# A graph and feed-forward layer: the first-layer products of the feed-forward moved between the two halves of the message sums

## The chip, the core and the metric

The kernel runs on one core of a Trainium2 chip. The metric is the device time of one execution in microseconds (us). The kernel is written with explicit semaphores: each engine (TensorE, VectorE or DVE, ScalarE or ACT, GpSimd or POOL, and SyncE or SP, which issues most DMAs) works through its own queue in program order and waits where the program says so.

## The reference

It is one layer over a graph of 6250 nodes with 256 features and 106,250 edges, sorted by target node.

```
xn = layernorm(x)
# graph attention, 4 heads of 64
h = xn @ W;  e = leaky_relu(a_src[src] + a_dst[dst]);  m = segment_max(e, dst)
ex = exp(e - m[dst]);  alpha = ex / segment_sum(ex, dst)[dst]
g = sigmoid(segment_sum(alpha * h[src], dst) + bias)
# linear attention with a gate
q, k, v = xn @ Wqkv;  k = softmax(k over nodes);  o = q @ (k^T v)
mix = (o * sigmoid(gelu(ln(xn) @ Wg1 + bg1) @ Wg2 + bg2)) @ Wproj + bproj
x = x + g + mix
# feed-forward on the nodes with the 3124 highest router weights of xn2
xn2 = layernorm(x);  r = xn2 @ wr + br
y = (gelu(xn2 @ w1 + b1) @ w2 + b2) * r     (256 -> 1024 -> 256)
out = x + xn2 + (y where selected, else 0)
```

Features, sums and weights are float32.

## The kernel before, in words

The nodes are 49 tiles of 128; the edges are 52 slices of 2048, each of four groups of 512 edges. A first part makes the node features and writes them to DRAM. The main part, on which the change bears, is one loop of 52 rounds over the slices (`steps`, which unrolls rounds 0 to 11 and 50 and 51 and repeats two rounds between). In a round k each engine runs a list of small functions in the order in which its `steps` call writes them out; every entry has a first and a last round. Node work trails edge work: a node tile is merged 5 rounds after its slice (LAG_MERGE), summed up after 6, its feed-forward's first layer runs from round 8 on (LAG_FF1), the second layer one round later.

What a round does for its edges:

- POOL (`fill`, L1014) gathers the feature rows of the next slices, 16 indirect DMAs in four batches g of four. Batch 0 waits for `scores_done` of TensorE, batch 1 for `scores_turned`, batch 2 for `max_turned`, batch 3 for `sums_done` of the first half of the sums. In the order of time a round has batch 3 (behind the first sums), batch 0, then batches 1 and 2.
- TensorE: `turn_scores` (L1824, instructions of L1833) transposes the edge scores; VectorE takes segment maxima by two scans; `turn_maxima` (L1842) transposes them back; VectorE makes differences (L1332, L1336), ScalarE their exponentials (L1615), VectorE the messages (L1352), four instructions, each 4 of the 16 tiles of gathered rows. TensorE sums the messages by target window (`window_sums`, L1873, instructions of L1882) in two halves, `first_sums` and `other_sums`, 16 instructions each. The first half waits for two of the four message products, the second for all four. Then `scores_ahead` (L1817) makes the target scores of the next slice.
- ScalarE, after the exponentials, runs `hidden` (L1670: the GELU of the first layer, four activations, L1675), then `keep_sums` (L1642: copies each half of the sums), `inverse_root` (L1625, L1627), the gates (L1656, L1660) and `keep_turned` (L1668).
- SP stores the copied sums to DRAM (L1091), loads the x tile (L1118) and the node tile (L1107, L1109), for which the stores must have landed.

The first layer of the feed-forward takes node tiles in pairs: 256 columns (two tiles) by 1024 hidden features. A round does half of the 1024, in two groups (`ff1_group`, L1909, instructions of L1917), eight instructions each, since a float32 product is two. In rounds of u = 0 (even k) both groups run in `other_ff1` (16 instructions). In rounds of u = 1 (odd k) the first group runs early, in `first_ff1`, between the transposes of scores and of maxima, and only the second one in `other_ff1` (8 instructions). The groups wait for GELUs of the round before, and the GELUs wait for `ff1_done`.

Of the kernel before, what the change touches and what calls it, by code (L numbers as in the profile page):

```python
# [73 lines left out]
def gps_layer(nc, x, src, dst, W, att_src, att_dst, gnn_bias, Wqkv, Wproj, bproj, ln_g, ln_b, Wg1, bg1, Wg2, bg2,  # L74
# [18 lines left out]
    with ExitStack() as ctx:  # L93
# [853 lines left out]
        def steps(eng, parts_of_body):  # L947

            loop_from = LAG_OUT + 2 + (LAG_OUT % 2)

            def body(k, u):
                for lo, hi, f in parts_of_body:
                    if lo <= (k if isinstance(k, int) else loop_from) < hi:
                        f(k - lo, (u - lo) % 2)
            for k in range(loop_from):
                body(k, k % 2)
            loop_to = NI - 2 - NI % 2
            with eng.Fori(loop_from // 2, loop_to // 2) as half:  # L960
                for u in range(2):
                    body(half * 2 + u, u)
            for k in range(loop_to, NI):
                body(k, k % 2)


        MAXIMUM = lambda f: (0, 1, f)
# [4 lines left out]
        SECOND = lambda f: (1, 5, f)  # L972
        LOAD_MIXER = lambda f: (0, 1, f)
        PREPARE = lambda f: (2, 3, f)
        CLEARS = lambda f: (0, NI - 2 - NI % 2, f)

        CONTEXT = lambda f: (0, 5, f)
        FOLD = lambda f: (5, 6, f)
        ROUNDS = 8

        EDGES = lambda f: (0, NI, f)
        AHEAD = lambda f: (0, NI - 1, f)
        NODE_AHEAD = lambda f: (LAG_MERGE - 1, NT + LAG_MERGE - 1, f)
        MERGE = lambda f: (LAG_MERGE, NT + LAG_MERGE, f)
        SUM = lambda f: (LAG_SUM, NT + LAG_SUM, f)
        LAST = NT + LAG_SUM - 1
        TURN = lambda f: (LAG_SUM, LAST, f)
        HALF = lambda f: (LAG_FF1, LAST, f)
        FF2 = lambda f: (LAG_FF1 + 1, LAST, f)
# [21 lines left out]
        with nc.Block() as block:  # L1011
# [715 lines left out]
            def _(pe):  # L1727
# [269 lines left out]
                def key_products():  # L1997
                    for i in range(EARLY, NT):
                        if i == EARLY + 12:
                            scores(0, 0)  # L2000
                        if i >= 2:
                            pe.wait_ge(S("keys_kept"), i - 1)
                        for t in range(CT):
                            mm = T.matmul(bank[5 + i % 2][:, 0:C], xnT[:, i, t * P:(t + 1) * P], wk_s[:, t, :],  # L2004
                                          start=(t == 0), stop=(t == CT - 1))
                        mm.then_inc(S("keys_done"), 1)

                def maximum(k, u):
# [6 lines left out]
                    for t in range(CT):  # L2015
# [2 lines left out]
                    mm.then_inc(S("max_across"), 1)  # L2018

                key_products()  # L2020
                steps(pe, [EDGES(turn_scores), FOLD(fold_turn), FF2(odd_ff2), HALF(first_ff1), EDGES(turn_maxima), SECOND(context_between), FOLD(fold_context), SUM(project), HALF(other_ff1),
                           EDGES(first_sums), EDGES(other_sums), AHEAD(scores_ahead), MAXIMUM(maximum), PREPARE(prepare), CONTEXT(context),
                           FF2(even_ff2),
                           FOLD(fold), MERGE(mixer), TURN(turn_normed)])
                last_tiles()
# [30 lines left out]
```

## Time and profile before

| | us |
|---|---|
| median of 3 runs (1601.31 to 1608.53) | 1608.32 |
| the profiled execution | 1624.43 |
| its span, from the first to the last instruction | 1622.4 |
| TensorE busy | 1151.6 (71%) |
| VectorE busy | 1021.9 (63%) |
| POOL busy | 854.7 (53%) |
| ScalarE busy | 513.3 (32%) |
| mean granted TensorE clock | 0.82 of full speed |

A line of the timeline has start, duration, engine, line of the program, operation, operands, the number of instructions merged into it, and in brackets the idle time of the engine before it with what ended it ("remote" is a semaphore that came from elsewhere and couldn't be tied to an instruction; "issue" is time for which the profile shows no wait). PE is TensorE. Of matmuls the trace has the start; their end is modelled. The trace lists when instructions ran, and the next instruction on another engine shows when it could see their completion.

### The profile page before, as it was taken

Reading aid. Unit: us, or ns where it says so; the run is one execution under the profiler, and the core shown is the slowest. Engines: PE = TensorE matmul, PEld = TensorE weight load, DVE = VectorE, ACT = ScalarE, POOL = GpSimd, SP = SyncE. Lnnn points to the kernel's source line nnn. Section 1 sums busy time; section 2 is a strip of 40 time slices with the busy share of each in tenths; the row PEclk is TensorE's granted clock in tenths of the full one; section 3 lists DMA queues with packets and bytes.
Section 4 is the critical chain, followed back from the end, with each engine's and each line's share of the span. In section 5 each row is a group of like instructions: output and inputs, shape, how many; then the busy total and the mean of one; then the engine's idle time right before and its main releaser. Section 6 shows DMA issues by size and latency. Waiting matters only on the chain.

```text
span 1622.4 us, 24002 instructions
## 1 busy us (share of the span) xinstructions
PE 1151.6 (71%) x5817; PEld 838.8 (52%) x5817; DVE 1021.9 (63%) x2596; ACT 513.3 (32%) x1155; POOL 854.7 (53%) x891
## 2 busy tenths in 40 slices
PE   6995667765667866777767677775778666776786
PEld 5753454543445554555445545554555544554565
DVE  6862455466666666665766566666666575766678
ACT  4542232103323333332333233333324232323341
POOL 0713455566565566665666565555656555555300
PEclk9997778865877877887779877887788878887889
DMA  9455355555554455455445444545555544444314
GB/s 250 114 107 142 121 146 152 150 138 132 139 135 123 132 129 132 129 129 136 124 129 131 131 122 126 134 121 130 135 132 131 129 129 124 129 123 128 92 32 159
DMA packets 165906, 212.04 MB, mean 131 GB/s; under 512 B 49524, under 2 KB 131252, under 8 KB 165704
## 3 DMA queue, kind: packets, MB, share of 16 engines
q0 software_dynamic: 39984, 110.94, 27.7%
q1 hardware_dynamic: 117570, 97.15, 21.2%
q10 hardware_dynamic: 8306, 3.41, 1.0%
q8 instruction: 19, 0.31, 0.1%
q14 instruction: 27, 0.22, 0.0%
HBM read 165.93 MB, written 45.46 MB: 130 GB/s over the span
## 4 chain that ended last, share of the span: by engine, by line
PE 24%; issue 23%; DVE 14%; another core or an unknown queue 11%; SPq 11%; ACT 3%; DMA 3%; DVEq 1%; POOL 0%; ACTq 0%; POOLq 0%
PE bank L1882 7%; PE bank L1917 5%; PE bank L1854 4%; SPq L1091 3%; SPq L1065 2%; PE bank L1733 2%; DVE ring L1352 2%; PE bank L2004 2%; PE bank L1893 2%; SPq L1051 2%; DVE forth L1320 1%; DVE srow L1323 1%; DVE xnT L1547 1%; DMA lists<-dloc_d 1%
## 5 line engine op out<-in xcount | busy, mean ns | idle before, releaser
L774 POOL DMA_INDIRECT ring<-feat_d,idx x832 | 816.4, 981 | 588.4 <-issue 419.9
L1882 PE MATMUL bank<-ring,hot 128*64 128x265 f32 x1664 | 251.2, 447 | 98.8 <-issue 65.8
L1882 PEld LDWEIGHTS bank<-ring,hot 128*64 128x64 f32 x1664 | 137.1, 157 | 204.2 <-issue 153.6
L1352 DVE TENSOR_TENSOR ring<-ring,bank 128x1024 f32<-128x1024 f32 x208 | 239.9, 1216 | 1.8 <-issue 1.4
L1917 PE MATMUL bank<-late,w_s 128*128 128x256 f32 x768 | 231.4, 462 | 0.4 <-ACT hT L1675 0.4
L1854 PE MATMUL bank<-w_s,hT 128*128 128x256 f32 x720 | 201.9, 443 | 20.8 <-DVE big L1345 15.8
L1917 PEld LDWEIGHTS bank<-late,w_s 128*128 128x128 f32 x768 | 182.5, 242 | 35.9 <-ACT hT L1675 0.5
L1854 PEld LDWEIGHTS bank<-w_s,hT 128*128 128x128 f32 x720 | 159.4, 227 | 52.6 <-DVE big L1345 16.0
L1833 PE MATMUL bank<-ident,lk 128*16 128x128 f32 x208 | 44.2, 352 | 185.2 <-issue 136.7
L1615 ACT ACTIVATE bank<-diff 128x64 f32<-128x64 f32 x52 | 11.8, 228 | 381.3 <-DVE diff L1336 250.3
L1675 ACT ACTIVATE hT<-bank,b_s 128x256 f32<-128x256 f32 x192 | 78.5, 472 | 150.6 <-remote 116.2
L1833 PEld LDWEIGHTS bank<-ident,lk 128*16 128x16 f32 x208 | 17.6, 103 | 202.0 <-issue 150.4
L1656 ACT ACTIVATE sc<-bank,hbg 128x128 f32<-128x128 f32 x98 | 30.5, 362 | 221.8 <-remote 208.2
L1332 DVE TENSOR_TENSOR ring<-bank,lastT 128x64 f32<-128x64 f32 x52 | 11.7, 225 | 129.6 <-remote 73.5
L1842 PE MATMUL bank<-ident,srow 16*128 16x16 f32 x208 | 33.0, 271 | 71.9 <-DVE srow L1323 50.9
L1320 DVE TENSOR_TENSOR_SCAN forth<-brk,bank 16x512 f32<-16x512 f32 x52 | 62.6, 1204 | 30.8 <-PE bank L1833 19.8
L1642 ACT ACTIVATE wout<-bank 128x265 f32<-128x265 f32 x104 | 38.2, 394 | 134.1 <-PE bank L1882 93.4
L1893 PE MATMUL bank<-wproj_s,sc 128*128 128x256 f32 x196 | 73.3, 509 | 6.1 <-DVE three L1424 3.3
L1842 PEld LDWEIGHTS bank<-ident,srow 16*128 16x128 f32 x208 | 28.7, 208 | 94.5 <-issue 94.5
L1389 DVE TENSOR_SCALAR late<-three,bn 128x256 f32<-128x256 f32 x47 | 20.7, 440 | 76.2 <-issue 41.2
L1249 DVE SCALAR_TENSOR_TENSOR sc<-sc,bank 128x256 f32<-128x256 f32 x49 | 20.4, 416 | 74.1 <-ACT sc L1656 74.1
L1267 DVE TENSOR_TENSOR hot<-bank,dlocT 128x512 f32<-128x512 f32 x104 | 66.4, 679 | 0.0
(284 smaller groups left out, 1808.2 us busy)
## 6 DMA issues: line engine op xcount, KB each, us to landing
parts_d<-zero SPq DMA_DIRECT2D x59, 265.0 KB
parts_d<-wout SPq DMA_DIRECT2D x208, 66.2 KB
lists<-dloc_d SPq DMA_DIRECT2D x104, 128.0 KB
ring<-feat_d,idx POOLq DMA_INDIRECT x832
parts<-parts_d SPq DMA_DIRECT2D x49, 265.0 KB
big<-in_x SPq DMA_DIRECT2D x7, 896.0 KB, 10.8
three<-in_x SPq DMA_DIRECT2D x49, 128.0 KB
out<-xnT SPq DMA_DIRECT2D x5, 896.0 KB, 4.2
```

The costliest lines, as they stand in the source:

```text
L774: pool.indirect_dma_start(out=ring[:, u * TI + q, 0:AW], out_offset=None, in_=feat_d, in_offset=bass.IndirectOffsetOnAxis(ap=idx[:, u, q:q ...
L1091: sp.dma_start(part_d[c][bass.ds(first[g], WIN), :], wout[c * WIN:(c + 1) * WIN, n, :]).then_inc(S(f"window_out{g % 2}"), 16)
L1267: V.tensor_tensor(hot[:, tiles, :], iota_ps.unsqueeze(1).to_broadcast([P, 2 * TG, WIN]), dlocT[:, bass.ds(k, 1), tiles].rearrange("p a q - ...
L1320: V.tensor_tensor_scan(forth[:, :], brk[:, 0:GE], bk_t[0:TI, :], LOWEST, ALU.add, ALU.max).then_inc(S("forth_made"), 1)
L1352: V.tensor_tensor(feats, feats, ex[:, g * TG:(g + 1) * TG, :].unsqueeze(3) .to_broadcast([P, TG, HEADS, HD]), ALU.mult).then_inc(S("scaled ...
L1675: A.activation(hT[:, 4 * u + m, :], bank[6 + m // 2][:, m % 2 * 2 * P:(m % 2 + 1) * 2 * P], ACT.Gelu_apprx_tanh, bias=b1_s[:, 4 * u + m:4 ...
L1833: mm = T.transpose(bk_t[0:TI, :].rearrange("r (e j) -> r j e", j=TG)[:, j, :], lk[:, u, j, :], ident[:, :])
L1842: mm = T.transpose(bk_e[:, MCOL + j * TI:MCOL + (j + 1) * TI], srow[:, :].rearrange("r (e j) -> r j e", j=TG)[:, j, :], ident[0:TI, 0:TI])
L1854: mm = T.matmul(to, hT[:, m, lo:lo + P], w2_s[:, m, :], start=(m == 0), stop=(m == FT - 1))
L1882: mm = T.matmul(bank[2 + n][c * WIN:(c + 1) * WIN, 0:SW], hot[:, q, :], ring[:, u * TI + q, 0:SW], start=(j == 0), stop=(j == TG - 1))
L1893: mm = T.matmul(bk_t[:, 0:C], sc[:, u, t * P:(t + 1) * P], wproj_s[:, t, :], start=(t == 0), stop=(t == CT - 1))
L1917: mm = T.matmul(bank[6 + g][:, m % 2 * 2 * P:(m % 2 + 1) * 2 * P], w1_s[:, t, m * P:(m + 1) * P], xn2T[:, t, :], start=(t == 0), stop=(t = ...
```

## The change

In TensorE's order of a round, `other_ff1` stood ahead of `first_sums`. Now it stands between `first_sums` and `other_sums`. Nothing else differs.

```diff
-                steps(pe, [EDGES(turn_scores), FOLD(fold_turn), FF2(odd_ff2), HALF(first_ff1), EDGES(turn_maxima), SECOND(context_between), FOLD(fold_context), SUM(project), HALF(other_ff1),
-                           EDGES(first_sums), EDGES(other_sums), AHEAD(scores_ahead), MAXIMUM(maximum), PREPARE(prepare), CONTEXT(context),
+                steps(pe, [EDGES(turn_scores), FOLD(fold_turn), FF2(odd_ff2), HALF(first_ff1), EDGES(turn_maxima), SECOND(context_between), FOLD(fold_context), SUM(project),
+                           EDGES(first_sums), HALF(other_ff1), EDGES(other_sums), AHEAD(scores_ahead), MAXIMUM(maximum), PREPARE(prepare), CONTEXT(context),
```

## Rows read from the trace of the kernel before

**Rows 1.** The costliest groups of the page: gathers and window sums.

```profile
L774 POOL DMA_INDIRECT ring<-feat_d,idx x832 | 816.4, 981 | 588.4 <-issue 419.9
L1882 PE MATMUL bank<-ring,hot 128*64 128x265 f32 x1664 | 251.2, 447 | 98.8 <-issue 65.8
```

**Rows 2.** Timeline of TensorE, 819 to 858 us: start, duration, line, count, idle before.

```profile
820.26 0.62 PE L1842 MATMUL bank<-ident,srow 16*128 16x16 f32 x4 [2.84 <-DVE srow L1323]
...
822.68 4.38 PE L1917 MATMUL bank<-late,w_s 128*128 128x256 f32 x16
826.99 3.80 PE L1882 MATMUL bank<-ring,hot 128*64 128x265 f32 x32
...
832.01 0.71 PE L1804 MATMUL bank<-hidT,wg_s 64*128 64x128 f32 x4
838.73 1.02 PE L1833 MATMUL bank<-ident,lk 128*16 128x128 f32 x4 [6.01 <-issue]
...
846.48 0.63 PE L1842 MATMUL bank<-ident,srow 16*128 16x16 f32 x4 [3.31 <-DVE srow L1323]
...
848.90 3.19 PE L1917 MATMUL bank<-late,w_s 128*128 128x256 f32 x8
852.03 4.21 PE L1882 MATMUL bank<-ring,hot 128*64 128x265 f32 x32
```

**Rows 3.** Timeline of VectorE, the same stretch: the message products.

```profile
821.98 4.61 DVE L1352 TENSOR_TENSOR ring<-ring,bank 128x1024 f32<-128x1024 f32 x4
...
848.20 4.62 DVE L1352 TENSOR_TENSOR ring<-ring,bank 128x1024 f32<-128x1024 f32 x4
```

**Rows 4.** Timeline of ScalarE, 829 to 846 us: the root and the gates.

```profile
831.39 1.28 ACT L1625 ACT_TABLE_LOAD   x1
...
834.29 0.20 ACT L1627 ACTIVATE bn<-bn 128x1 f32<-128x1 f32 x1
842.85 0.63 ACT L1656 ACTIVATE sc<-bank,hbg 128x128 f32<-128x128 f32 x2 [8.36 <-remote]
```

**Rows 5.** Timeline of POOL, the same stretch: its gathers.

```profile
830.92 0.95 POOL L774 DMA_INDIRECT ring<-feat_d,idx  x1 [2.53 <-PE bank L1882]
...
839.67 0.95 POOL L774 DMA_INDIRECT ring<-feat_d,idx  x1 [0.30 <-issue]
843.83 0.94 POOL L774 DMA_INDIRECT ring<-feat_d,idx  x1 [3.21 <-issue]
```

**Rows 6.** Timeline of a late round: TensorE, VectorE, then POOL.

```profile
896.88 1.89 PE L1917 MATMUL bank<-late,w_s 128*128 128x256 f32 x8
905.59 5.74 PE L1882 MATMUL bank<-ring,hot 128*64 128x265 f32 x32 [6.81 <-issue]
911.25 0.36 PE L1817 MATMUL bank<-stat,lists 128*128 128x24 bf16 x8
...
903.18 4.62 DVE L1352 TENSOR_TENSOR ring<-ring,bank 128x1024 f32<-128x1024 f32 x4
...
910.35 0.95 POOL L774 DMA_INDIRECT ring<-feat_d,idx  x1 [4.36 <-PE bank L1882]
...
914.11 0.94 POOL L774 DMA_INDIRECT ring<-feat_d,idx  x1 [0.30 <-issue]
917.57 0.95 POOL L774 DMA_INDIRECT ring<-feat_d,idx  x1 [2.52 <-issue]
```

**Rows 7.** Busy time by stretch; the column after POOL is the granted clock.

```profile
896.90:898.80 1.90, 1.87 (x9) 1.31 (x7) 0.00 (x0) 0.00 (x0) 0.95 (x1) 1.00 0.40 81
905.60:909.40 3.80, 3.80 (x18) 2.16 (x20) 3.04 (x4) 0.78 (x3) 0.39 (x1) 0.50 0.62 199
```

**Rows 8.** Waits of the whole run: total us, times, longest.

```profile
ACT sc L1656 <- remote: 208.2, 32, 8.9
...
POOL ring L774 <- PE bank L1882: 114.0, 40, 5.1
...
PE bank L1882 <- DVE ring L1352: 32.7, 11, 5.2
```

## The prediction

> **What bounds the kernel now.** I began with the costliest groups of the page. A round takes one slice of 2048 edges, and no engine is full in it: the gathers on POOL and the window sums of TensorE (L1882) are its first two entries, and the idle time beside them is mostly called "issue" [rows 1]. So the answer isn't in a share. I then read one pair of neighbouring rounds engine by engine in the timeline.
>
> On TensorE a round goes from one transpose of the maxima to the next: 820.26 to 846.48, 26.2 us [rows 2]. Behind the maxima come the projection, the first layer (16 instructions in one round, 8 in the next, since the other 8 stand early in that round), the 32 window sums, the scores of the next round, the mixer and the gates. VectorE multiplies the messages in that time, four instructions in 4.61 us [rows 3], and the first sums need only two of them.
>
> The row that counts is on ScalarE. The gates' matmuls end at 832.72 on TensorE [rows 2], yet the activation that reads them starts at 842.85, after 8.36 us of a wait put down to "remote" [rows 4]. POOL explains when: eight gathers run without a gap from 830.92, the last ends at 840.62, and ScalarE goes on 2.2 us after that [rows 4, 5]. POOL itself, waiting for the turned scores that TensorE finished at 839.75, starts its next eight at 843.83 [rows 2, 5]. So while gathers are under way, a completion of TensorE can reach the others up to ten microseconds late; it gets through when the burst has drained. Two bursts of eight at 1.25 us, each with 2.2 us of draining and about 1.0 us until POOL acts, make 2 x 12.9 = 25.8 us, which is the round that I see (26.2). In 32 of the calls of the gates such a wait appears, 208.2 us in all [rows 8].
>
> What decides whether a completion is held is where it falls in a burst. Now the second half of the sums ends at 830.79, before POOL has begun the burst that the first half releases at 830.92; it gets through, ScalarE takes its table at 831.39 for the logarithm of the variance, and the reciprocal root is there at 834.49 [rows 2, 4, 5]. From there VectorE normalises, adds up the scores, and TensorE turns them at 838.73 [rows 2]. That is 7.9 us from the second sums to the turned scores, of which nothing can start earlier: ScalarE and VectorE are in program order.
>
> **The change part by part.** No instruction is added or removed, and no DMA, semaphore or wait. On TensorE's queue 8 or 16 first-layer instructions move behind the first 16 sums. No queue of SP or POOL is touched, but both wait on what moves.
>
> *The first sums come earlier.* In the round of sixteen, two messages are ready at 821.98 + 2 x 1.15 = 824.3; the sums start at 826.99 today because the first layer is in front [rows 2, 3]. They would start 2.7 us earlier, and TensorE, which reaches the first layer at 822.68, would stand still for 1.6 us. In the round of eight, 848.20 + 2.3 = 850.5 against 852.03: 1.5 us earlier with 1.6 us of idle time [rows 2, 3]. What does it buy? POOL's third batch waits for the first sums, 40 times in all for 114.0 us [rows 8]. But half the sums end at 826.99 + 1.9 = 828.9 today and POOL starts at 830.92, 1.1 us more than its usual 1.0 us later: their completion is already held by the burst before [rows 2, 5]. Bounds: 0, and 1.5 us in each of half the 44 rounds, 33 us. I take 10 us of gain, near the zero of the row.
>
> *The second sums come later.* They end when 16 sums, the first layer and 16 sums have run from the new start: 824.3 + 1.9 + 4.4 + 1.9 = 832.5 against 830.8, and 850.5 + 1.9 + 3.2 + 2.1 = 857.7 against 856.2 [rows 2]. That is 1.7 and 1.5 us, the idle time opened ahead of the first sums. At the lower granted clock, 0.50 of full speed (1.2 GHz), 32 sums take 5.74 us instead of the 3.80 at full speed (2.4 GHz), and eight first-layer instructions take 1.89 us at full speed, twice that at half [rows 2, 6, 7]. A new idle hole can bring that state, so I take 1.9 us as the mean. ScalarE adds to it: the four GELUs of the first layer stand ahead of the copy of the first sums on its queue, so the earlier first sums aren't stored earlier, and SP's stores of windows, which wait for that copy, and its load of the node tile behind them, move later with it.
>
> Where does this lie on the path? Three kinds of round:
>
> (a) Late rounds, 11 of them by the waits of the sums for the messages [rows 8]. The example has its first layer done at 898.77, and the messages start only at 903.18, so the sums start at 905.59 after TensorE has stood for 6.8 us [rows 6]. There the first layer is free today. Moved, it runs wholly on the path: 1.89 us for eight, 3.6 for sixteen, to twice these at the low clock. Eleven at 2.8 us, the middle of 1.9 and 3.6: 31 us. If its cover stays gone at the low clock it is 60.
>
> (b) Rounds where the gates come through in time: 49 tiles less the 32 that wait, less five outside the 44 rounds that have a first layer (three rounds ahead of them, two tiles behind), 12 [rows 8]. There the way over the root and the turned scores sets the end, and a delay of the second sums counts in full: 12 x 1.9 = 23 us.
>
> (c) The 21 others. The turned scores are ready at 839.75 and aren't seen before 842.8, so 3.1 us are spare [rows 2, 4] and 1.9 us vanish in it. But here the second sums now end at 3 to 5 us behind the first ones, instead of 1.9, that is 2 to 4 us into POOL's new burst. The trace has the case of a completion that falls there: in the late round the scores' products end at 911.61, 1.3 us into a burst that starts at 910.35, POOL stops after four gathers for want of them, and goes on at 917.57, so that they were held for 5.0 us [rows 6]. Nothing before shows the second sums themselves that deep in a burst. Bounds for a round: 0 (as at 830.79, just ahead of the burst) and 5.0 us of hold plus 1.7 us of GELUs that then stand ahead of the copy, less the spare 3.1: 3.6 us. The rounds of sixteen are nearer to the upper end, those of eight to zero. I take 1.5 us for the ten of sixteen: 15 us.
>
> The sum: 31 + 23 + 15 - 10 = 59 us. The profiled execution took 1624.4 us (span 1622.4, 2.0 around it), so it would take 1683; it lies 16 us above the median of the timed runs, 1608.3, and there the same sum gives 1667.
>
> The Trainium skill speaks of completions (TensorE: Matmul & The Clock Gate, "The cost: per-tile semaphore tail"): an increment is a write that costs some 26 ns, and the last matmul's one is enough, since matmuls end in order. The gates' row has 10.1 us between end and reader, so the trace doesn't agree while gathers run. By that rule no completion is ever held, and the sum is that of the first rival below.
>
> **The rivals.**
>
> *Only the direct delay, without holds.* Completions of the second sums slip through, as they do at 830.79. Then (a) and (b) stay, less the 10 us: 44 us, 1652. For it: TensorE is only 2 to 4 us into the burst. Against it: the scores held at 1.3 us.
>
> *Holds in nearly every round.* Late second sums break the long burst: four gathers, a gap, four more. At 3.6 us in 40 rounds it is 144 us, 1752. For it: the 5.0 us of the late round. Against it: in (c) the gates would then come through earlier, at the end of the shorter burst.
>
> *All is absorbed.* The round is two bursts of POOL, 25.8 us, whatever TensorE does within; late rounds shift so that their node tile is no longer waited for. 1608. Against it: 11 rounds with idle TensorE ahead of the messages, where the first layer is free now.
>
> *It gets faster.* The first sums' completion, 1.5 to 2.7 us earlier, gets out before it would be held, and POOL starts its third batch sooner. If 22 rounds gain 1.5 us and the second sums stay within the spare 3.1: -33 us, 1575. It decides from the point where the first sums end before the burst begun by the turned scores (843.83) holds them; they would end at 852.4, 8.6 us into it, as against 10.3 us today [rows 2, 5], and the gates of the row are held in all of a burst, so I see little for it.
>
> **How the numbers follow.** Forecast 0.46, direct delay only 0.18, holds in nearly every round 0.13, absorbed 0.12, faster 0.11. A measurement can tell about 0.5% (8 us) from no change. Slower: 0.46 + 0.18 + 0.13 = 0.77, nearly all over 0.5%; I put 0.76. Within 0.5%: 0.13. Faster: 0.11. The likeliest case alone has 1635 to 1705 (each term between its bounds, not all at one end). The range goes on to the many holds on one side, 1740, and to the absorbed case on the other, 1604.
>
> **What would show it.** Right: TensorE idle between projection and first sums in ordinary rounds; in the late rounds the second sums later by the whole first layer; more of POOL's bursts of four instead of eight; ScalarE's copy of the second sums, and with it the table load of the root, waiting for a completion that came late; more waits of VectorE's scores. Wrong: POOL's gathers starting sooner behind the first sums with rounds shorter than 25 us; or the wait of the gates, 208.2 us now, growing by just what the rest lost, which would be the absorbed case. If the granted clock falls much below 0.82 and the rounds lengthen in TensorE's rows themselves, the size would have another cause than the one I sum.

## The result, and the profile after

The kernel became slower: 1639.11 us (median of 4 runs, 1631.94 to 1647.85) against 1607.53 us (4 runs, 1601.31 to 1608.53), ratio 1.0199 with a 95% interval of 1.0163 to 1.0236. That is 31.6 us, 0.7 us for each of the 44 rounds with a first layer. The prediction had 1667 and a range of 1604 to 1740: right in sign and range, and its sum of 59 us was almost twice what was measured. The two profiled executions are only 14 us apart (1624.43 and 1638.36), since the one of before lies above its median.

Two groups of the page of the changed kernel, with busy time, mean, and idle time before:

```profile
L774 POOL DMA_INDIRECT ring<-feat_d,idx x832 | 814.1, 978 | 598.3 <-issue 454.7
L1882 PE MATMUL bank<-ring,hot 128*64 128x265 f32 x1664 | 269.0, 473 | 148.8 <-issue 80.7
```

The same 1664 sums take 18 us more of TensorE, and it stands 50 us more ahead of them [rows 1]. A round of sixteen in the timeline of TensorE:

```profile
1144.77 0.63 PE L1842 MATMUL bank<-ident,srow 16*128 16x16 f32 x4 [3.37 <-DVE srow L1323]
1145.33 2.08 PE L1893 MATMUL bank<-wproj_s,sc 128*128 128x256 f32 x4
1148.99 3.47 PE L1882 MATMUL bank<-ring,hot 128*64 128x265 f32 x16 [1.59 <-issue]
1152.39 3.72 PE L1917 MATMUL bank<-late,w_s 128*128 128x256 f32 x16
1156.05 2.01 PE L1882 MATMUL bank<-ring,hot 128*64 128x265 f32 x16
...
1159.27 0.71 PE L1804 MATMUL bank<-hidT,wg_s 64*128 64x128 f32 x4
1165.22 1.02 PE L1833 MATMUL bank<-ident,lk 128*16 128x128 f32 x4 [5.24 <-issue]
```

The idle hole is there (1.59 us), and the first 16 sums behind it take 3.47 us where the second 16 take 2.01. The granted clock, in the column after POOL, of the projection ahead of the hole, of the first sums and of the time behind them:

```profile
1145.30:1147.40 2.10, 2.10 (x5) 1.18 (x4) 1.77 (x7) 1.19 (x4) 1.49 (x3) 0.50 0.39 80
1148.90:1151.90 3.00, 2.91 (x14) 1.72 (x16) 2.99 (x4) 0.00 (x0) 2.12 (x3) 0.50 0.89 229
1151.90:1156.20 4.30, 4.30 (x23) 3.15 (x22) 3.77 (x13) 0.89 (x3) 1.89 (x2) 0.99 0.27 80
```

Half speed (1.2 GHz) in the first sums, full speed (2.4 GHz) behind them. In this round the clock was low before the hole already, behind the wait of 3.37 us ahead of the maxima. So it was in the round of [rows 2]: there the first layer ran in it (0.50 over 820.80 to 824.20), and it was back at full speed for the sums (1.00 over 826.99 to 830.79). Here the low clock lasts through the hole and into the sums. ScalarE of that round:

```profile
1154.46 0.84 ACT L1675 ACTIVATE hT<-bank,b_s 128x256 f32<-128x256 f32 x2 [6.35 <-PE bank L1917]
1156.15 0.84 ACT L1675 ACTIVATE hT<-bank,b_s 128x256 f32<-128x256 f32 x2 [0.86 <-PE bank L1917]
1156.88 0.39 ACT L1642 ACTIVATE wout<-bank 128x265 f32<-128x265 f32 x1
1158.24 0.39 ACT L1642 ACTIVATE wout<-bank 128x265 f32<-128x265 f32 x1 [0.97 <-PE bank L1882]
1158.65 1.28 ACT L1625 ACT_TABLE_LOAD   x1
...
1161.66 0.61 ACT L1656 ACTIVATE sc<-bank,hbg 128x128 f32<-128x128 f32 x2
```

The first sums were done at 1152.5, and their copy comes at 1156.88, behind the GELUs. The second sums end at 1158.06; the table load of the root (its first instruction) starts 13.9 us behind the maxima (1144.77), where the round in [rows 2, 4] had 11.1. But the gates' activation, which waited for 8.36 us there, waits for nothing here. The waits of the whole run:

```profile
ACT sc L1656 <- remote: 100.8, 15, 8.1
POOL ring L774 <- PE bank L1882: 74.3, 32, 3.6
PE bank L1882 <- DVE ring L1352: 67.9, 21, 7.5
DVE mg L1275 <- DMA hidT<-hid_d: 1.3, 1, 1.3
```

Against [rows 8]: the gates' late completions fell from 208.2 us to 100.8, POOL's waits for the first sums from 114.0 to 74.3, and the sums' own wait for the messages rose from 32.7 to 67.9. The line for VectorE's wait for the node tile was 8.9 us in 7 waits before.

Means over the timelines of both kernels, rounds 8 to 50, in us behind the first transpose of the maxima (worked out from each round's rows; "root" is the start of the activation of L1625, behind its table load; the last column is the distance to the next round's maxima):

| | first sums start | second sums end | root | turned scores | gates on ScalarE | round |
|---|---|---|---|---|---|---|
| sixteen, before | 6.3 | 11.1 | 13.2 | 19.2 | 18.9 | 25.0 |
| sixteen, changed | 5.0 | 13.9 | 16.8 | 22.1 | 18.6 | 26.3 |
| eight, before | 6.7 | 12.1 | 14.4 | 20.7 | 22.5 | 27.9 |
| eight, changed | 4.4 | 11.8 | 14.1 | 19.8 | 21.2 | 27.1 |

In the rounds of sixteen the second sums, the root and the turned scores are 2.8 to 3.6 us later, the gates 0.3 us sooner, and the round is only 1.3 us longer. The rounds of eight didn't get longer in this pair of profiles.

### The profile page after: what moved, and what is told of

Read it like the earlier page. It is cut to its first block, busy times and chain, and to the rows that moved or that the text cites. A ratio compares the mean times of both kernels' runs of the same rounds, so it can differ in the third digit from the quotient of the medians.

```text
span 1636.2 us, 24002 instructions
## 1 busy us (share of the span) xinstructions
PE 1151.2 (70%) x5817; PEld 818.5 (50%) x5817; DVE 1018.4 (62%) x2596; ACT 511.6 (31%) x1155; POOL 852.4 (52%) x891
## 3 DMA queue, kind: packets, MB, share of 16 engines
q1 hardware_dynamic: 117570, 97.15, 20.7%
## 4 chain that ended last, share of the span: by engine, by line
PE 34%; issue 22%; DVE 17%; another core or an unknown queue 8%; ACT 6%; SPq 3%; DMA 2%; DVEq 1%; ACTq 0%
PE bank L1882 12%; PE bank L1917 9%; PE bank L1733 4%; DVE ring L1352 3%; PE bank L1854 3%; ACT L1625 3%; DVE forth L1320 2%; DVE srow L1323 2%; PE bank L1833 2%; PE bank L2004 2%; DMA parts_d<-wout 1%; DVE hot L1267 1%; PE bank L1842 1%; DVE xnT L1547 1%
## 5 line engine op out<-in xcount | busy, mean ns | idle before, releaser
L774 POOL DMA_INDIRECT ring<-feat_d,idx x832 | 814.1, 978 | 598.3 <-issue 454.7
L1882 PE MATMUL bank<-ring,hot 128*64 128x265 f32 x1664 | 269.0, 473 | 148.8 <-issue 80.7
L1917 PE MATMUL bank<-late,w_s 128*128 128x256 f32 x768 | 226.0, 452 | 0.4 <-ACT hT L1675 0.4
L1854 PE MATMUL bank<-w_s,hT 128*128 128x256 f32 x720 | 197.1, 435 | 23.8 <-DVE big L1345 20.6
L1917 PEld LDWEIGHTS bank<-late,w_s 128*128 128x128 f32 x768 | 171.3, 232 | 54.5 <-issue 25.5
L1854 PEld LDWEIGHTS bank<-w_s,hT 128*128 128x128 f32 x720 | 155.9, 222 | 53.5 <-DVE big L1345 16.2
L1615 ACT ACTIVATE bank<-diff 128x64 f32<-128x64 f32 x52 | 11.8, 228 | 393.1 <-DVE diff L1336 229.6
L1332 DVE TENSOR_TENSOR ring<-bank,lastT 128x64 f32<-128x64 f32 x52 | 11.7, 225 | 100.0 <-PE bank L1842 45.6
L1893 PE MATMUL bank<-wproj_s,sc 128*128 128x256 f32 x196 | 65.8, 465 | 6.5 <-DVE three L1424 3.3
L1656 ACT ACTIVATE sc<-bank,hbg 128x128 f32<-128x128 f32 x98 | 30.1, 358 | 118.2 <-remote 100.8
L1323 DVE TENSOR_TENSOR_SCAN srow<-brk,forth 16x512 f32<-16x512 f32 x52 | 63.4, 1220 | 1.8
L713 PE MATMUL bank<-late,xnT 128*128 128x328 f32 x196 | 63.7, 452 | 0.7 <-ACT xnT L604 0.7
```

The costliest lines, as they stand in the source:

```text
L774: pool.indirect_dma_start(out=ring[:, u * TI + q, 0:AW], out_offset=None, in_=feat_d, in_offset=bass.IndirectOffsetOnAxis(ap=idx[:, u, q:q ...
L1323: V.tensor_tensor_scan(srow[:, :][:, ::-1], brk[:, 1:GE + 1][:, ::-1], forth[:, :][:, ::-1], LOWEST, ALU.add, ALU.max).then_inc(S("max_mad ...
L1854: mm = T.matmul(to, hT[:, m, lo:lo + P], w2_s[:, m, :], start=(m == 0), stop=(m == FT - 1))
L1882: mm = T.matmul(bank[2 + n][c * WIN:(c + 1) * WIN, 0:SW], hot[:, q, :], ring[:, u * TI + q, 0:SW], start=(j == 0), stop=(j == TG - 1))
L1893: mm = T.matmul(bk_t[:, 0:C], sc[:, u, t * P:(t + 1) * P], wproj_s[:, t, :], start=(t == 0), stop=(t == CT - 1))
L1917: mm = T.matmul(bank[6 + g][:, m % 2 * 2 * P:(m % 2 + 1) * 2 * P], w1_s[:, t, m * P:(m + 1) * P], xn2T[:, t, :], start=(t == 0), stop=(t = ...
```

## The experiments

Ratios are to the kernel before, timed on the same chip. The experiments ran on three chips, and these differ: the kernel before took 1624.8 us on the first (the four experiments down to the copy ahead of the GELUs), 1606.3 on the second (down to the first layer behind both sums) and 1334.5 on the third (the last four). So ratios are compared across chips only with that in mind.

**The rounds apart.** `other_ff1` was divided by kind of round, each put ahead of `first_sums` or behind:

```diff
-  SUM(project), EDGES(first_sums), HALF(other_ff1), EDGES(other_sums),
+  SUM(project), HALF(eight_ff1), EDGES(first_sums), HALF(sixteen_ff1), EDGES(other_sums),
```

> The first layer moves between the halves of the sums only in the rounds of sixteen; the rounds of eight keep the order of before. Theory A (the end of the second sums moves back, and ScalarE's GELUs with it, mostly in the rounds of sixteen: 11.1 us behind the maxima before, 13.9 changed): this alone brings nearly all of the loss, 1.6 to 2.6% over the kernel before. Rival B (the idle hole ahead of the first sums and the lower clock behind it, which both kinds of round get alike): about half, 0.8 to 1.2%.

> The first layer moves only in the rounds of eight; the rounds of sixteen keep the order of before. Theory A: no loss or a small gain, -0.8 to +0.4%, since the second sums of these rounds end at 11.6 us behind the maxima in the changed trace and at 12.0 in the one of before. Rival B (idle hole and clock): a loss of 0.8 to 1.2%.

Measured: only the sixteen moved, 1.0053 (1.0028 to 1.0077); only the eight moved, 1.0082 (1.0053 to 1.0112). Theory A, which I had drawn from the two profiles, fell: the smaller move costs no less than the large one. 0.5% is under what rival B asked for the sixteen, its 0.8% for the eight is met. Together they are 1.35%, the whole change 2.0% on other chips; whether they add up on one chip wasn't measured. What both theories left out shows in the trace of the second: in its rounds of eight ScalarE's copy of the second sums starts 2.1 us behind their end on the mean, where it is 0.35 in the kernel before, and ScalarE stands idle meanwhile. The completion comes late there.

**Half of the sixteen ahead.** The first eight of sixteen stay in front, in the time in which TensorE would stand:

```diff
+  SUM(project), HALF(half_of_sixteen), EDGES(first_sums), HALF(rest_of_sixteen), EDGES(other_sums),
```

> In the rounds of sixteen the first eight first-layer instructions stay ahead of the first sums, where TensorE would wait for the messages anyway (1.8 us of work into 2.4 us of wait), and the other eight stand between the halves; the rounds of eight as before. Theory A: the second sums end where they ended before, so the time is that of before within 0.5%, or up to 0.5% faster. Rival C (any completion of the first layer that comes behind the first sums holds up ScalarE's copy of them and the stores behind it): 0.8 to 1.5% slower.

Measured: 1.0017 (0.9995 to 1.0039), within the 0.5% of theory A, and rival C fell. Useful work in the hole, and the move costs nothing that can be told; it gains nothing either.

**The copy ahead of the GELUs**, in the changed kernel:

```diff
-  MERGE(merge_exp), HALF(hidden), ..., EDGES(keep_sums),
+  MERGE(merge_exp), EDGES(keep_first), HALF(hidden), ..., EDGES(keep_second),
```

> The changed kernel with one edit on ScalarE: the copy of the first sums stands ahead of the four GELUs, the copy of the second sums behind them. Theory C (the GELUs of the first layer, which now end later, hold up the copy of the first sums, SP's stores and the node tile): most of the 2% comes back, 0 to 0.7% over the kernel before. Theory A in its narrow form (only the end of the second sums on TensorE counts): still 1.5 to 2.3% slower than before.

Measured: 1.0266 (1.0238 to 1.0293). Theory C fell; even the narrow theory was exceeded. In its timelines the copy of the first sums is 4.2 us earlier in the rounds of sixteen (8.9 against 13.1) and the round isn't shorter (26.6). Storing the first sums earlier doesn't bring the time back. But the edit also has a price of its own: ScalarE now waits 251.9 us for completions of sums put down to "remote" (30 times), where it was 30.7 us (5 times) in the changed kernel, and in the rounds of eight the second copy starts 1.4 us later (13.8 against 12.4). What the order of the stores alone is worth isn't shown.

**The changed kernel again, and without the third batch of gathers.** The changed kernel was timed once more as it is. Then, in both orders, POOL leaves out the gathers of batch 3, and VectorE its wait for them (not shown), so that a quarter of the edges are summed from stale rows:

```diff
 for g in range(GI):
+    if g == 3 and not known_below(k, 2):
+        continue
```

> The changed kernel itself, to stand beside the others on one chip. If the moves in the two kinds of round add up, 0.5% + 0.8% = 1.3% over the kernel before; if they work on each other by their bursts, 1.8 to 2.4%.

> The order of before, with the gathers of batch 3 (those that POOL issues behind the first sums) left out from slice 2 on, 200 of 832 gathers; a quarter of the edges are summed from stale rows. Only its distance to the next kernel counts. Theory H (the cost of the change is that the second sums' completion falls into the burst that the first sums release): the two differ by less than 0.5%. Rival D (the cost is the later end of the second sums on TensorE and nothing of POOL's): the changed order is 1.3 to 2.5% slower here too. The time itself: 5 to 12% under the kernel before, since a burst of four is gone from each round.

> The changed order with the same gathers left out, so that a quarter of the edges are summed from stale rows. Theory H: within 0.5% of the one before. Rival D: 1.3 to 2.5% slower than it; with POOL's part of the round shorter even 3%, since less of TensorE's way is hidden.

Measured: changed 1.0206 (1.0166 to 1.0246); without batch 3 the order of before 0.8714 (1399.99 us), the changed order 0.9478 (1521.35 us). The changed order is 8.7% slower there, 121 us or 2.8 us a round. This decides against theory H as it was put: with the burst gone that the first sums release, the cost of the change is 3.6 times as large (121 us against 33.7), not nil. It doesn't show that such holds cost nothing where the burst is there. The order of before (TensorE):

```profile
722.53 1.13 PE L1895 MATMUL bank<-wproj_s,sc 128*128 128x256 f32 x4
723.50 3.62 PE L1919 MATMUL bank<-late,w_s 128*128 128x256 f32 x16
727.05 3.12 PE L1884 MATMUL bank<-ring,hot 128*64 128x265 f32 x25
730.78 1.13 PE L1884 MATMUL bank<-ring,hot 128*64 128x265 f32 x7 [0.62 <-issue]
```

and the changed order:

```profile
723.22 1.13 PE L1895 MATMUL bank<-wproj_s,sc 128*128 128x256 f32 x4
727.03 3.70 PE L1884 MATMUL bank<-ring,hot 128*64 128x265 f32 x16 [2.68 <-issue]
730.65 3.72 PE L1919 MATMUL bank<-late,w_s 128*128 128x256 f32 x16
734.30 2.01 PE L1884 MATMUL bank<-ring,hot 128*64 128x265 f32 x16
```

From the projection's start the second sums end 9.4 us later in the one (731.91) and 13.1 us in the other (736.31). The 3.7 us are the hole (2.68) and the low clock behind it (3.70 for sixteen sums instead of 2.01), with 0.6 us of a wait gone. On average over the rounds the second sums end 2.8 us later in the rounds of sixteen and 3.2 in those of eight, and the rounds are 2.8 and 2.5 us longer: here nearly the whole delay arrives at the end.

**The first layer behind both sums.**

```diff
-  EDGES(first_sums), HALF(other_ff1), EDGES(other_sums), AHEAD(scores_ahead),
+  EDGES(first_sums), EDGES(other_sums), AHEAD(scores_ahead), HALF(other_ff1),
 (ScalarE)
-  HALF(hidden), ..., EDGES(keep_sums), SUM(inverse_root), MERGE(gates),
+  ..., EDGES(keep_sums), SUM(inverse_root), HALF(hidden), MERGE(gates),
```

> The first layer of other_ff1 stands behind both halves of the sums and the scores ahead, and ScalarE's GELUs behind the reciprocal root. Theory A (what counts is when the second sums and the root behind them end): the sums end near 8.3 us behind the maxima, where they ended at 11 to 12, and the kernel is 0.5 to 2% faster than before. Rival E (POOL's bursts set the round, and the turned scores were seen late anyway): within 0.5%. Rival F (the gates and the second layer come later by the first layer that now stands ahead of them): 0.5 to 1.5% slower.

Measured: 1.0675 (1.0631 to 1.0718). Rival F had the sign, at several times its price. In the rounds of eight the second layer of the same round waits for the GELUs, with the gates and the turned scores queued behind it:

```profile
954.83 1.97 PE L1917 MATMUL bank<-late,w_s 128*128 128x256 f32 x8
961.80 6.63 PE L1854 MATMUL bank<-w_s,hT 128*128 128x256 f32 x16 [5.00 <-ACT hT L1675]
968.27 1.05 PE L1797 MATMUL bank<-xnT,wqc_s 128*128 x8
```

The second sums ended 0.9 us earlier than in the kernel before (11.2 against 12.1 in the rounds of eight), and these rounds were 32.3 us long.

**The hole filled.** In front of `first_sums` TensorE computes eight first-layer instructions whose results are overwritten by the real ones afterwards:

```diff
-  SUM(project), EDGES(first_sums), HALF(other_ff1),
+  SUM(project), HALF(filler), EDGES(first_sums), HALF(other_ff1),
```

> The changed order without the gathers of batch 3 (a quarter of the edges summed from stale rows, as in no_third_after), and in TensorE's idle time ahead of the first sums eight first-layer instructions more, whose result is overwritten by the real ones. It does 8 instructions of useless work in each of 44 rounds. Theory G (the hole lets the granted clock fall, so that the first 16 sums take 3.7 us instead of 1.9): the first sums run at 1.9 to 2.2 us and the kernel is faster than no_third_after by 1 to 1.8 us a round, 45 to 80 us, ratio to before 0.90 to 0.925. Rival I (the idle time itself is the cost, the clock isn't): no gain, 0.945 to 0.96.

> The changed kernel with the same eight useless instructions in the hole, all gathers in place. Theory G with POOL's bursts hiding two thirds of what TensorE loses: 0.5 to 1.3% slower than before, where the changed kernel is 2.0% slower. Rival I: 2.0 to 3% slower.

Measured, without batch 3 and then with all gathers: 1.0455 (1.0425 to 1.0485) and 1.0530 (1.0502 to 1.0558), on the chip on which the kernel before takes 1334.5 us. Neither ratio fits what I had written, since both rest on a chip that holds completions. The clock's part can be read all the same. The filled kernel, in a round of sixteen:

```profile
707.07 1.89 PE L1937 MATMUL bank<-late,w_s 128*128 128x256 f32 x8
709.81 2.01 PE L1882 MATMUL bank<-ring,hot 128*64 128x265 f32 x16 [0.86 <-DVE ring L1352]
711.75 3.72 PE L1917 MATMUL bank<-late,w_s 128*128 128x256 f32 x16
715.40 2.01 PE L1882 MATMUL bank<-ring,hot 128*64 128x265 f32 x16
```

```profile
709.80:711.80 2.00, 1.99 (x17) 1.14 (x17) 2.00 (x2) 0.00 (x0) 1.69 (x2) 1.00 0.72 166
```

With the hole down to 0.86 us the first sums run at full clock. Over rounds 8 to 50, from the start of the first of the 16 first sums to the modelled end of the last, 31 of 43 took more than 2.6 us in the changed kernel (mean 3.13), and 11 of 43 in the kernel before (mean 2.46), all eleven behind holes of 3.0 us or more. In the filled kernel it is 1 of 43 (mean 2.05), and that one is round 8, which has no filler and a hole of 1.6 us. In the kernel of the next paragraph that waits for the second sums, which has the hole open and ran on this same chip, 31 of 43 did (mean 3.07). So open holes bring the low clock into the sums. In 24 of the 31 the clock was still full when the hole began; in 7, the round shown above among them, it was low already and stayed so. Not every hole does it: 12 of 43 had one and kept full speed.

What is left when the clock is whole is 70 us or 1.6 us a round (5.3% of 1334.5). The filler hardly adds to it: the first sums start 4.3 us behind the maxima with it, and 4.2 to 4.3 without it in the kernel of the next paragraph. The rest is the delay of the second sums. Against the kernel of small rows below, which has the order of before on this chip, they end 3.0 us later in the rounds of sixteen (12.0 against 9.0) and 1.2 in those of eight, and the rounds are 2.7 and 0.8 us longer. The unfilled changed kernel wasn't timed on this chip.

**Smaller gathers, and another pace.** One kernel is the order of before with rows of 24 bytes instead of 1040 gathered, the other the changed kernel with one number changed in POOL's waits:

```diff
 if g == 3 and not known_below(k, LAG_FF1):
-    used = number(pool, NB * (k - 1) + 1)
+    used = number(pool, NB * (k - 1) + 2)
```

> The order of before with the gathers from slice 2 on reading rows of 24 bytes (another table) in place of 1040; as many gathers, waits and instructions, but the edges are summed from stale rows. Theory of the hold by traffic (a completion of TensorE is held while the gathers' data are under way): ScalarE's waits of the gates under remote shrink below 50 us and the round falls below 23 us, ratio 0.82 to 0.92. Rival J (the hold comes with POOL's issuing of gathers, whatever they carry): waits of the gates stay near 200 us and the round near 25 us, ratio 0.96 to 1.0.

> The changed kernel, with batch 3 of the gathers waiting for the second sums instead of the first. Theory H' (holds of the second sums matter in the full kernel): ScalarE's copy of the second sums follows their end by 0.6 us, 1.6 us today in the rounds of sixteen, and what POOL loses is at most regained: 1 to 3% slower than before. Theory K (what POOL's round costs is set by when the first sums let batch 3 go): 5 to 10% slower, since batch 3 starts 2 to 5 us later.

Measured: 0.9856 (0.9812 to 0.9899) and 1.1628 (1.1578 to 1.1677). The first tells nothing of its two theories: on this chip no completion is held whatever is gathered, as the next section shows. The second has the sign of theory K at about twice its price: POOL waits 241.3 us for the second sums (44 waits), and its third batch starts that much later. With the third batch let go by the first sums POOL's waits for them are 7.0 us on this chip, as the filled kernel shows below.

## Why the prediction was right, and where it was not

The total lay well inside a range of 136 us. But the largest term of the sum had the wrong sign, so that the total came out near is in part luck.

*The first sums come earlier.* Right, by 1.3 us in the rounds of sixteen and 2.3 in those of eight on average, where I had 2.7 and 1.5 from one round each. That POOL would get little of it was right too: its wait for them fell by 40 us, and its idle time as a whole rose from 588.4 to 598.3.

*The second sums come later, by 1.9 us.* Mis-sized. In the rounds of sixteen it is 2.8, in those of eight they end 0.3 us sooner, since none of these is late any more. Against the rounds that weren't late before (10.0 and 10.3 us behind the maxima) those that aren't late now (13.1 and 11.8) end them 3.1 and 1.5 us later. I had named the low clock and not counted it as the normal case: 31 of 43 first halves ran in it against 11 before, 0.7 us a round on the mean (3.13 against 2.46). The filled kernel shows that the open hole brings it. The GELUs ahead of the copy are there as foretold, and moving the copy in front of them didn't help.

*(a) The late rounds, 31 us.* Wrong, and this is the step that failed most: it took the number of late rounds as fixed. Before, 12 of 43 rounds had messages that started more than 4.5 us behind the maxima; in the changed kernel 4, none of them a round of eight. I hadn't asked what made them late. It is a held completion: VectorE's differences (L1332) wait for the turned maxima. In the late round of [rows 6] TensorE had them at 895.99:

```profile
895.33 0.66 PE L1842 MATMUL bank<-ident,srow 16*128 16x16 f32 x4
...
897.07 0.95 POOL L774 DMA_INDIRECT ring<-feat_d,idx  x1 [0.30 <-issue]
...
900.48 0.23 DVE L1332 TENSOR_TENSOR ring<-bank,lastT 128x64 f32<-128x64 f32 x1 [5.74 <-remote]
902.48 0.17 DVE L1275 TENSOR_SCALAR mg<-parts 128x2 f32<-128x2 f32 x1 [1.65 <-DMA hidT<-hid_d]
```

POOL's burst ends at 898.02 and the differences start 2.5 us behind it; the node tile adds 1.65 us. Over the whole run, before and then changed:

```profile
DVE ring L1332 <- remote: 73.5, 12, 7.7
DVE ring L1332 <- remote: 23.2, 4, 6.4
```

In every late round of both kernels the burst outlasts the turned maxima. A short round (22.4 to 23.6 us, the one ahead of each first late round before) brings its successor's maxima into POOL's burst. Waits for the node tile are a small part, 8.9 us and now 1.3. When the rounds of sixteen grew, fewer maxima fell into a burst, and the messages of all 43 rounds start 44 us earlier in sum. In the four late rounds that are left the whole first layer stands behind the messages, as foretold. Where the messages start equally late (6.4 to 6.7 us behind the maxima, two rounds of sixteen in each kernel), the second sums end at 18.0 and 18.1 us against 15.6 and 15.8: 2.3 us later, not the 3.6 of the whole first layer. What a round of sixteen lost, the round of eight behind it got back in part: 25.0 + 27.9 = 52.9 against 26.3 + 27.1 = 53.4 us. This succession is read from the traces; no experiment took it apart.

*(b) and (c), what is on the path and what is spare.* The picture fits. Where the bursts are shortened nearly all of the later end of the second sums arrives (no third batch, 2.8 us a round, 121 us); where they stand, 0.7 us a round (31.6 us). How much of the rest went into the spare time, 3.1 us in the one round that I had read, and how much into the late rounds isn't taken apart. The gates' wait shrank from 208.2 to 100.8 us as the turned scores became what is late.

*Holds of the second sums, 15 us.* The mechanism is there. POOL's bursts did break into fours, 72 of them against 37 before in rounds 8 to 50; in the round shown in the result section, gathers run from 1155.26 and again from 1161.98:

```profile
1159.02 0.95 POOL L774 DMA_INDIRECT ring<-feat_d,idx  x1 [0.30 <-issue]
1161.98 1.04 POOL L774 DMA_INDIRECT ring<-feat_d,idx  x1 [2.01 <-issue]
```

ScalarE stood idle for more than 0.6 us between the end of the second sums and their copy in 18 of these 43 rounds, 15 of them of sixteen, and in 3 before. The copy starts 1.2 us behind the end of the second sums in the rounds of sixteen (0.3 before) and 0.6 in those of eight (0.35 before): some 25 us in all. Whether this reaches the end of the round isn't shown: without the third batch the copy follows at once (0.17 us) and the change costs more, so it isn't the whole cost; how large a part it is stays open. A broken burst also lets the gates through sooner, which I had written down only against the rival of many holds.

*The rivals.* "Only the direct delay" came nearest with 1652. On the third chip ScalarE's copy of the second sums starts 0.05 to 0.19 us behind their modelled end in every round from 8 to 50 of the filled kernel; on the others completions are held while gathers run. The Trainium skill (TensorE: Matmul & The Clock Gate, "The cost: per-tile semaphore tail") has an increment in tens of nanoseconds. The third chip's trace doesn't speak against that, the others' don't agree with it. "All is absorbed" had seen that the late rounds would shift, though by the node tile, which was the smaller cause. "Faster" and "holds in nearly every round" didn't come.

## What to carry to other kernels

Work that stands ahead of a wait is worth what it covers: taken out from under the wait it costs its hole, and then the clock that falls in the hole. Before moving a block of matmuls, leave as much of it in front as the wait is long; with half of the sixteen left in front, the cost of the move in the rounds of sixteen went from 0.53% to 0.17%, which can't be told from nothing. And don't price rounds that are late today as if their lateness were fixed, since it can be the echo of the short round ahead: first look what they wait for.

## What the runs showed of the hardware

How long a completion of TensorE takes to be seen while indirect gathers run differs from one chip to another in these runs. On those of the first results and the first two of the experiments it is held, up to 10.1 us in [rows 2, 4], and the kernel before takes 1606 to 1625 us. On the third the same program takes 1334.5 us (1328.91 to 1344.14, 11 runs), and in none of the four kernels profiled there have ScalarE's gates a wait under "remote" in the view of waits. No one kernel was profiled on both sorts of chip, so the difference in the traces is read from different programs, and that in the time from the same one. In the filled kernel POOL's waits for the sums are 7.0 us instead of 74.3, with all its gathers in place:

```profile
PE bank L1882 <- DVE ring L1352: 42.7, 46, 3.3
POOL ring L774 <- PE bank L1882: 7.0, 23, 0.3
```

There leaving out a quarter of the gathers changes little (1395.12 against 1404.56 us, both filled), while on the second chip it took 13% from the kernel before and 7% from the changed one. The hold isn't of TensorE's completions alone: between 837.1 and 842.1 us of the kernel before, in and just behind the burst of [rows 5], SyncE's register instructions take 0.7 us each, where their median is 0.03 to 0.04 us; in the filled kernel none takes more than 0.18 us. What the chips differ in, no run shows, and whether the hold goes with the gathers' bytes or with their issue is open, because the experiment for it ran on the chip without holds.
